# Where the shift-3 maximum lives: SBUF for both users, or PSUM for the minimum and an SBUF copy for the sum

## What is computed

```
for shift in (1, 3):
    o1 = cen - neighbour at 4 offsets, o2 = cen - neighbour at the 4 opposite offsets
    outs.append(min over the 4 directions of o1 * o2)
out = max(outs) + mean(outs)
g = pointwise(depthwise3x3(out))
result = cen * sigmoid(g) + cen
```

## Time and profile before

| what | before |
|---|---|
| time, median of 3 runs | 118.89 us (118.88 to 118.97) |
| span of the profiled execution | 116.7 us |
| VectorE busy | 97.5 us (84%), 129 instructions |
| GpSimd busy | 84.2 us (72%), 55 |
| TensorE busy | 82.3 us (71%), 915 |
| ScalarE busy | 57.9 us (50%), 102 |

### The profile page before, as it was taken

One profiled execution on the slowest core, in us unless ns is written; L12 is line 12 of the kernel. 1 busy time (PEld: TensorE's weight loads), 2 busy tenths in 40 slices (PEclk: granted clock), 3 DMA queues, 4 the chain that ended last, 5 costly groups with the idle time before them and its releaser, 6 DMA issues.

```text
span 116.7 us, 2294 instructions
## 1 busy us (share of the span) xinstructions
PE 82.3 (71%) x915; PEld 41.9 (36%) x915; DVE 97.5 (84%) x129; ACT 57.9 (50%) x102; POOL 84.2 (72%) x55
## 2 busy tenths in 40 slices
PE   2999999997999600779900599900589993559970
PEld 1295997774878300313200122300122331012440
DVE  5065099999999999999999999999999989999031
ACT  5000255626573854533359543336754039699570
POOL 7000089992999999999999999999999973400400
PEclk9999999999999996569996579995557999557999
DMA  3999000000000089700019860002986000988045
GB/s 81 339 348 321 14 6 0 6 0 0 6 3 6 3 157 192 224 0 0 0 28 229 258 147 6 0 0 48 228 276 200 0 0 21 228 252 246 11 135 135
DMA packets 10013, 12.12 MB, mean 104 GB/s; under 512 B 2036, under 2 KB 7188, under 8 KB 9876
## 3 DMA queue, kind: packets, MB, share of 16 engines
q1 hardware_dynamic: 10004, 11.99, 37.4%
HBM read 3.17 MB, written 2.10 MB: 45 GB/s over the span
## 4 chain that ended last, share of the span: by engine, by line
DVE 46%; PE 28%; issue 10%; DMA 7%; SPq 3%; ACT 2%; POOL 1%; DVEq 0%; POOLq 0%; ACTq 0%
DVE m L502 16%; DVE slots L491 12%; PE acc L637 12%; DMA early<-att 7%; DVE u L205 5%; PE acc L558 5%; DVE att L532 4%; PE acc L586 3%; PE slots L609 3%; SPq L354 3%; DVE att L509 3%; PE slots L637 2%; PE slots L566 2%; DVE m L488 2%; ACT cen L399 1%
## 5 line engine op out<-in xcount | busy, mean ns | idle before, releaser
L205 POOL TENSOR_TENSOR u<-cen 128x1120 f32<-128x1120 f32 (+9 forms) x41 | 75.4, 1878 | 14.1 <-ACT cen L399 14.1
L412 ACT ACTIVATE slots<-u 128x1024 f32<-128x1024 f32 (+2 forms) x48 | 35.2, 745 | 41.2 <-DVE m L502 20.7
L491 DVE TENSOR_TENSOR slots<-slots,u 128x1024 f32<-128x1024 f32 (+2 forms) x36 | 30.8, 870 | 0.6 <-ACT slots L412 0.3
L637 PE MATMUL acc<-early,wc 128*32 128x512 f32 x168 | 23.8, 720 | 10.2 <-DMA early<-att 10.2
L502 DVE TENSOR_TENSOR m<-slots,m 128x1024 f32<-128x1024 f32 (+2 forms) x33 | 29.5, 895 | 0.4
L586 PE MATMUL acc<-early 128*32 128x256 f32 (+1 forms) x640 | 28.3, 337 | 0.8 <-ACT cen L399 0.8
L558 PE MATMUL acc<-eye 128*128 128x512 f32 x18 | 14.1, 923 | 18.7 <-ACT early L422 8.7
L586 PEld LDWEIGHTS acc<-early 128*32 128x32 f32 x640 | 23.0, 137 | 6.4 <-issue 2.3
L637 PEld LDWEIGHTS acc<-early,wc 128*32 128x32 f32 x168 | 5.7, 130 | 29.3 <-issue 15.2
L293 POOL TENSOR_TENSOR early<-early,cen 128x512 f32<-128x512 f32 (+1 forms) x4 | 6.8, 1703 | 11.2 <-ACT early L422 11.2
L558 PEld LDWEIGHTS acc<-eye 128*128 128x128 f32 x18 | 4.2, 263 | 23.9 <-issue 11.3
(11 more groups left out here) (29 smaller groups left out, 34.9 us busy)
## 6 DMA issues: line engine op xcount, KB each, us to landing
early<-att SPq DMA_DIRECT2D x28, 204.0 KB, 3.5
early<-in_x_dram SPq DMA_DIRECT2D x2, 1024.0 KB, 8.5
early<-in_L_conv_g_weight_dram SPq DMA_DIRECT2D x1, 1024.0 KB, 4.9
out_dram<-early SPq DMA_DIRECT2D x2, 512.0 KB, 3.9
early<-eye SPq DMA_DIRECT2D x1, 816.0 KB, 6.9
out_dram<-early SPq DMA_DIRECT2D x3, 256.0 KB, 2.4
out_dram<-early SPq DMA_DIRECT2D x2, 128.0 KB, 2.1
wc<-w_tap SPq DMA_DIRECT2D x1, 36.0 KB, 2.8
```

The source lines that it names most:

```text
L205: return eng.tensor_tensor(u[j][:, r0 - base:r1 - base, g], cen[:, PAD + r0:PAD + r1, g, left:left + wide], cen[:, PAD + r0 - dy:PAD + r1 ...
L412: nc.scalar.activation(slot_px(j, t), ahead(j, t), ACT.Copy).then_inc(u_copied, 1)
L491: nc.vector.tensor_tensor(slot_px(j, t), slot_px(j, t), here(j, t), ALU.mult).then_inc(multiplied, 1)
L637: last = nc.tensor.matmul(at[C * q:C * (q + 1)], weights[:, i, :], src[:, y0:y0 + r1 - r0, :, i:i + W], start=i == 0, stop=i == TAPS - 1)
```

## The change

The maximum of plane 7 (the last of shift 3) of the steps in `PE_SUMS` goes to plane 7's PSUM slot instead of `m3`. ScalarE copies it to `m3` (`keep_m3`, right behind the next step's first plane copy), and TensorE adds from that copy. The minimum (`take_least`) reads `m1` in SBUF and plane 7's slot in PSUM, and stands one multiply later, behind the next step's multiply of plane 0. `m1` has two buffers, by the parity of t, so that multiply no longer waits. The sum's slot is now slot 1, and there are two tables of slots: `SLOT_AFTER_SUM` for steps 3, 4 and 5, `SLOT_ALONE` for steps 0, 1 and 2. To make room for the second `m1`, the stage of units of index 1 lies in the third window, and the copies that fill that window wait for its store.

```diff
-    SLOT = (0, 1, 0, 2, 1, 0, 2, 1)
-    SUM_SLOT = 2
+    SLOT_ALONE = (0, 1, 2, 0, 1, 1, 0, 2)
+    SLOT_AFTER_SUM = (0, 0, 1, 2, 0, 1, 0, 2)
+    SUM_SLOT = 1
...
-        early = sb("early", [P, stage_at + N_STAGES * G * K * W])
+        early = sb("early", [P, stage_at + (N_STAGES - 1) * G * K * W])
...
+        stage_places = [stage_at, 2 * IN_WINDOW, stage_at + G * K * W]
+        stage = [early[:, at:at + G * K * W] for at in stage_places]
...
-        m1 = sb("m1", [P, G * K * W])
+        m1 = [sb(f"m1_{i}", [P, G * K * W]) for i in range(2)]
...
+        def slot_no(j, t):
+
+            return (SLOT_AFTER_SUM if t - 1 in PE_SUMS else SLOT_ALONE)[j]
...
+            elif i == NP - 1:
+                eng.wait_ge(least, t - PE_SUMS[0] + 1)
...
+            def keep_m3(t):
+
+                act.wait_ge(compared, n_compared(NP - 1, t))
+                nc.scalar.activation(m3[:, 0:pixels(t)], slot(NP - 1, t), ACT.Copy).then_inc(m3_kept, 1)
...
                     copy_ahead(j, t)
+                    if j == 0 and t - 1 in PE_SUMS:
+                        keep_m3(t - 1)
...
+            act.wait_ge(stored[1], 16)
...
-                    m = (m1, m3)[j // ND]
-                    if j == 0 and t - 1 in PE_SUMS:
-
-                        dve.wait_ge(m1_summed, t - PE_SUMS[0])
-                        dve.wait_ge(least, t - PE_SUMS[0])
+                    m = (m1[t % 2], m3)[j // ND]
...
-                dst = slot(j, t) if j == NP - 1 and t not in PE_SUMS else m[:, 0:n]
+                dst = slot(j, t) if j == NP - 1 else m[:, 0:n]
...
+            def take_least(t):
+
+                dve.wait_ge(m3_kept, t - PE_SUMS[0] + 1)
+                dve.wait_ge(compared, n_compared(NP - 1, t))
+                nc.vector.tensor_tensor(att_px(t), packed(m1[t % 2], t), slot_px(NP - 1, t), ALU.min).then_inc(least, 1)
...
-                for what, j in (("m", 0), ("m", 1), ("finish", t - 1), ("x", 1), ("m", 2), ("m", 3), ("x", 2),
-                                ("m", 4), ("x", 3), ("m", 5), ("m", 6), ("x", 5), ("m", 7), ("x", 6), ("x", 7)):
+                for what, j in (("m", 0), ("least", t - 1), ("m", 1), ("finish", t - 1), ("x", 1), ("m", 2), ("m", 3),
+                                ("x", 2), ("m", 4), ("x", 3), ("m", 5), ("m", 6), ("x", 5), ("m", 7), ("x", 6),
+                                ("x", 7)):
...
-                if t in PE_SUMS:
-                    nc.vector.tensor_tensor(att_px(t), packed(m1, t), packed(m3, t), ALU.min).then_inc(least, 1)
-                    continue
...
-                for m in (m1, m3):
+                for m in (m1[t % 2], m3):
                     if m is m3:
-                        pe.wait_ge(compared, n_compared(NP - 1, t))
+                        pe.wait_ge(m3_kept, t - PE_SUMS[0] + 1)
```

More of the change, by code:

```diff
@@ L122, in build @@
                   for i in range(N_WINDOWS)]
-        stage = [early[:, stage_at + i * G * K * W:stage_at + (i + 1) * G * K * W] for i in range(N_STAGES)]
+        stage_places = [stage_at, 2 * IN_WINDOW, stage_at + G * K * W]
+        stage = [early[:, at:at + G * K * W] for at in stage_places]
         stage += [early[:, i * BANK:(i + 1) * BANK] for i in range(max(STAGE_OF) + 1 - N_STAGES)]
@@ L170, in build @@
         compared = sem("compared")
-        m1_summed = sem("m1_summed")
         summed = sem("summed")
         least = sem("least")
+        m3_kept = sem("m3_kept")
         weighed = sem("weighed")
@@ L222, in packed @@
             return ap[:, 0:pixels(t)].rearrange("p (y g x) -> p y g x", g=S_IMGS[t][1] - S_IMGS[t][0], x=W)
+        def slot_no(j, t):
+            return (SLOT_AFTER_SUM if t - 1 in PE_SUMS else SLOT_ALONE)[j]
         def slot(j, t):
-            return slots[:, SLOT[j] * 2 * BANK:SLOT[j] * 2 * BANK + pixels(t)]
+            return slots[:, slot_no(j, t) * 2 * BANK:slot_no(j, t) * 2 * BANK + pixels(t)]
         def slot_px(j, t):
@@ L234, in wait_slot @@
         def wait_slot(eng, j, t):
-            before = [i for i in range(j) if SLOT[i] == SLOT[j]]
+            own = slot_no(j, t)
+            before = [i for i in range(j) if slot_no(i, t) == own]
             if not before and t == 0:
@@ L239, in wait_slot @@
                 return
-            if not before and t - 1 in PE_SUMS and SLOT[j] == SUM_SLOT:
+            if not before and t - 1 in PE_SUMS and own == SUM_SLOT:
                 eng.wait_ge(att_ready, t)
                 return
-            i, t = (before[-1], t) if before else (max(i for i in range(NP) if SLOT[i] == SLOT[j]), t - 1)
+            i, t = (before[-1], t) if before else (max(i for i in range(NP) if slot_no(i, t - 1) == own), t - 1)
             if i == NP - 1 and t not in PE_SUMS:
                 eng.wait_ge(att_ready, t + 1)
+            elif i == NP - 1:
+                eng.wait_ge(least, t - PE_SUMS[0] + 1)
             elif i % ND == 0:
@@ L527, in _ @@
                     elif t - 1 in PE_SUMS:
-                        finish(t - 1)
+                        (take_least if what == "least" else finish)(t - 1)
+                if t in PE_SUMS:
+                    continue
                 n = pixels(t)
                 dve.wait_ge(compared, n_compared(NP - 1, t))
-                if t in PE_SUMS:
-                    nc.vector.tensor_tensor(att_px(t), packed(m1, t), packed(m3, t), ALU.min).then_inc(least, 1)
-                    continue
-                nc.vector.scalar_tensor_tensor(m3[:, 0:n], m1[:, 0:n], 3.0, slot(NP - 1, t), ALU.mult,
+                nc.vector.scalar_tensor_tensor(m3[:, 0:n], m1[t % 2][:, 0:n], 3.0, slot(NP - 1, t), ALU.mult,
                                                ALU.add).then_inc(weighed, 1)
-                nc.vector.scalar_tensor_tensor(slot(NP - 1, t), slot(NP - 1, t), 3.0, m1[:, 0:n], ALU.mult,
+                nc.vector.scalar_tensor_tensor(slot(NP - 1, t), slot(NP - 1, t), 3.0, m1[t % 2][:, 0:n], ALU.mult,
                                                ALU.add).then_inc(weighed, 1)
@@ L544, in _ @@
                     dve.wait_ge(att_ready, T)
+                    dve.wait_ge(stored[1], 16)
                 for dst, src in last_part(n):
@@ L602, in add_maxima @@
                     warm(WARM_BEFORE_SUM[t], conv_bank(0))
-                pe.wait_ge(compared, n_compared(max(i for i in range(NP) if SLOT[i] == SUM_SLOT), t))
-                for m in (m1, m3):
+                pe.wait_ge(compared, n_compared(max(i for i in range(NP) if slot_no(i, t) == SUM_SLOT), t))
+                for m in (m1[t % 2], m3):
                     if m is m3:
-                        pe.wait_ge(compared, n_compared(NP - 1, t))
+                        pe.wait_ge(m3_kept, t - PE_SUMS[0] + 1)
                     for b0, b1 in banks:
                         last = nc.tensor.matmul(slots[:, SUM_SLOT * 2 * BANK + b0:SUM_SLOT * 2 * BANK + b1], ident,
-                                                m[:, b0:b1], start=m is m1, stop=m is m3)
-                    last.then_inc(m1_summed if m is m1 else summed, 1)
+                                                m[:, b0:b1], start=m is not m3, stop=m is m3)
+                last.then_inc(summed, 1)
             def convolve(s):
```

## The result

The changed kernel takes 120.98 us (median of 4 runs, 120.96 to 121.17) against 118.93 (118.88 to 119.58) for the kernel before in the same comparison: ratio 1.016, 95% interval 1.0135 to 1.019. It is slower by 2.05 us; 121.0 was predicted, with +2.07. The span grows from 116.7 to 118.9 us. Some executions of any kernel here run several per cent longer than its others; ratios and intervals leave them out, medians and the ranges beside them don't.

A forecast was written before the change was run, and what follows sets the result against it. VectorE was taken to bound almost without a gap up to about 80 us, then a chain through transfers and TensorE. Late part -2.2 plus early loss 4.27 gave +2.07 on 118.89: 121.0 us, range 116.4 to 121.5.

The forecast's parts named there:

- The first collision: Step 1: GpSimd's subtraction starts 0.08 us ahead of VectorE's of plane 4, which must wait for it; cost 2.24 us.
- rival A: At the first collision VectorE keeps the port, so the whole late gain shows: 116.7 us, chance 0.27.
- The second collision: Step 2: GpSimd's subtraction of plane 5 is ahead of VectorE's of plane 2; total early loss becomes 4.27 us.
- The tie of step 0: Step 0: VectorE's subtraction started 0.01 us ahead of GpSimd's and kept its 0.73 us; read as who goes first.
- The late part: Steps 3 to 5 and the tail: cheaper minima and earlier `finish`, worth -2.2 us, bounds -1.6 and -2.6.
- the prediction's own sign, that `finish` waits for TensorE: Late steps: `finish` was to be covered by 0.2 us; its waiting for TensorE would show the late part wrong.
- Rival C: Late sums: TensorE idles 1.5 us between halves, slows, and `finish` loses 1.4 us in a step; chance 0.04.
- the minimum at 1.22 us: Steps 2 and 3: with one PSUM operand the minimum falls from 2.60 and 2.54 us to 1.22.
- plane 4's multiply late by 0.45 in step 4: Step 4: ScalarE's copies and gate instructions after `finish(3)` make plane 4's multiply lose 0.45 us.
- `finish(4)` 2.14 us after ScalarE's copy ends: Step 5: copy to 91.96, then the `m3` half of the sum, `finish(4)` starting at 94.11.
- 9.58 us from `finish(4)` to the end of step 5: Tail: with gate 2 between copies after `finish(4)`, VectorE's step 5 ends only 0.5 us sooner, at 104.9.

The follow-up runs named there:

- e1: The changed kernel with plane 2's copy of step 1 again waiting for plane 0's multiply: 116.27 us, ratio 0.979 to the kernel before.
- e4: The changed kernel with an unneeded 128x1 ScalarE copy between plane 2's copy of step 1 and the move behind it: 117.10 us.
- e3: The changed kernel with GpSimd's subtraction of plane 5 of step 2 waiting for VectorE's of plane 2: 118.84 us.
- e2: The kernel before with the new slot table in steps 0 and 1 alone: 122.89 us, ratio 1.025.
- e7: The kernel of e1 with gate 1 on ScalarE behind plane 4 of step 4 instead of plane 3: 116.04 us.
- e9: The kernel of e1 with gate 1 behind plane 4 of step 4 and gate 2 behind plane 4 of step 5: 116.49 us.
- e10: The kernel of e1 run once more, unchanged, on the same chip as e9: 116.58 us.
- e6: The kernel of e1 with gate 2 on ScalarE behind plane 4 of step 5 instead of plane 2: 115.91 us.
- e8: The changed kernel with two GpSimd subtractions, plane 7 of step 0 and the first of step 2, waiting for VectorE subtractions: 116.96 us.
- e11: The kernel of e1 with the minimum reading m3 from ScalarE's SBUF copy, run again for its profile: ratio 1.002 to the kernel before.

## Why the prediction was right

**The first collision.** Predicted: the move 0.46 us sooner, GpSimd 0.08 ahead, 2.24 us lost. Measured in the changed kernel: GpSimd 0.08 ahead (28.03 and 28.11), 3.02-0.73 = 2.29 lost. Removed by a wait (e1) and by a delay (e4), which leaves what rival A describes: 116.3 and 117.1 us, against 116.7.

**The second collision.** Predicted: GpSimd ahead by 0.06, 2.03 more. Measured: ahead by 0.04, 3.55-1.44 = 2.11; removed alone by e3, worth 2.1 in time. Calling GpSimd ahead here was the weakest step, and e2 shows how weak: less than 0.01 us, where e7 and e9 show that a GpSimd ahead by so little can also lose.

**An early term that was missing.** The tie of step 0 was read as evidence for who goes first, and not as a race that could turn. In the changed kernel it cost 0.63 us at 18.7 and gave back 0.43 at 26.3: 0.2 net. It is chance, and no effect of the change: e1 and e10 lost the tie, e6, e7 and e9 won it, and in step 0 these five kernels are the same.

**The late part.** Predicted -2.2, bounds -1.6 and -2.6. By the ruler the changed kernel's step 2 ends at 43.09 us (57.36-14.27) against 38.54 before, 4.55 later, and the whole 2.63 later: the late part gave 1.9 us. In e1_wait_back it gave 2.4. The difference lies with TensorE. Timelines of TensorE, after and in e1_wait_back:

```profile
67.79 8.20 PE L656 MATMUL acc<-early,wc 128*32 128x512 f32 x48 [4.62 <-DMA early<-att]
75.92 3.70 PE L628 MATMUL slots<-m,eye 128*128 128x512 f32 x8
```

```profile
63.46 7.05 PE L658 MATMUL acc<-early,wc 128*32 128x512 f32 x48 [4.62 <-DMA early<-att]
70.44 1.98 PE L630 MATMUL slots<-m,eye 128*128 128x512 f32 x4
72.66 1.98 PE L630 MATMUL slots<-m,eye 128*128 128x512 f32 x4 [0.24 <-ACT m L428]
```

Strips 1 and 2 took 8.20 us in the changed kernel and 7.05 in e1_wait_back, at a mean granted clock of 0.65 and 0.76: the lower level lasted for 5.8 and 3.4 us of them. So the sum of step 3 ran into `finish(3)`, which waited 0.34 us. By the prediction's own sign, that `finish` waits for TensorE, the late part was wrong here. The idling before these strips was 4.62 us in both profiles, so it doesn't explain the difference; what does stays open. Rival C had the right engine but the wrong place: behind the idling between the halves of the sum (0.74 us in the changed kernel, 1.61 in e6) the `m3` half took 1.98 us, at the full clock. The other terms held: the minimum at 1.22 us, plane 4's multiply late by 0.45 in step 4 (85.95: the 0.35 of the row, and 0.09 by which VectorE's instructions overlap elsewhere; e7 confirms it), `finish(4)` 2.14 us after ScalarE's copy ends (2.15 predicted), and 9.58 us from `finish(4)` to the end of step 5 (9.6).

**The sum.** -2.2+4.27 = +2.07 stood against a measured +2.05. That agreement is in part luck, since the terms agree less well: 4.37 for the two collisions, 0.18 for the tie, -1.92 for the late part, which make +2.63, and the profiled execution of the changed kernel began its subtractions 0.55 us sooner, which no edit explains. That the early loss goes through to the end does hold: against e1_wait_back the changed kernel is 4.36 us behind at the end of step 2 (43.09 against 38.73 by the ruler) and 4.81 at the end.

## What to carry to other kernels

When two engines share a port that one holds for a whole instruction, look for pairs of starts that lie close together before freeing anything upstream: an engine with slack that starts 0.1 us sooner can cost the critical engine its whole instruction. An edit's early and late effects can be told apart by giving back one wait. And a tie won is not a gain until it is clear what the loser, now late, runs into next.

## What the runs showed of the hardware

- Who starts clearly first has the port. GpSimd ahead of VectorE by 0.20 us (before, 26.0), 0.08 (changed kernel), 0.07 (e2), 0.04 (e8 at 26.0; changed kernel, 37.5): VectorE waited each time. VectorE ahead by 0.01 (before, 19.3; e4, 29.2) or 0.4 (e1, 28.1): GpSimd waited.
- With GpSimd ahead by 0.02 us or less it went either way: VectorE waited six times (the tie of step 0 in the changed kernel, e1, e3, e4 and e10; e2 at 37.3) and went first twice (the tie in e7 and e9). The Trainium skill (SBUF — State Buffer, section Who interferes with whom) says that issue order decides who blocks. From 0.04 us on these profiles agree; below that the starts that they show don't give the order.
- Which of the two goes first makes a large difference to the kernel: VectorE lost 2.3 us when a subtraction of 2.5 us was ahead of its one of 0.7. The other way round GpSimd, which has slack, lost 0.6 us (3.12 against 2.51 in e4; 1.35 against 0.76 in step 0), and 0.2 when VectorE led by 0.4 (2.71 in e1).
- A VectorE instruction that reads one operand from PSUM never waited for GpSimd in any profile: none of size 128x1024 took over 1.23 us, and the minimum took 1.22 each time, also beside GpSimd subtractions, against 1.56 to 2.85 us for the same minimum from SBUF (e11).
